# Two-batch transformer-and-state-space block on one core: setup work moved from ahead of batch 0 into its attention, x loaded early, two of three query spreading copies moved to POOL

## What is computed

```
0 attention: q, k, v = x@wq, x@wk, x@wv (16 query heads on 4 key heads, 16 wide), rotary;
             out = 0.5 * (softmax(causal) @ v + softmax(local, window 32) @ v);  out @ wo
1 feed-forward: w1, w2 = ternary(W_fc), ternary(W_proj)  (groups of 64 weights, scale = mean |w|)
             h = relu(x @ w1.T)**2;  rms_norm(h) @ w2.T
2 state-space mixer: in-projection, softplus time steps, 64 heads of 8, state 64, chunks of 64 tokens,
             gate silu(z), rms_norm, out-projection
3 rank mixer: x @ sum of 8 factors of 256x256, plus bias
```

## Time and profile before

| | |
|---|---|
| median of three runs (lowest, highest) | 1797.98 us (1793.96, 1803.11) |
| the profiled execution | 1803.51 us, of which its span is 1801.7 us |
| busy: PE, PEld, DVE | 1399.0 us (78%), 811.3 us (45%), 1166.2 us (65%) |
| busy: ACT, POOL | 924.9 us (51%), 277.8 us (15%) |
| mean granted TensorE clock | 0.861 of full speed |
| DMA | 63.29 MB, mean 35 GB/s |

### The profile page before, as it was taken

The page is one execution under the profiler, slowest core; times in us unless marked ns, Lnnn a source line. Parts: engine busy times, 40 slices in busy tenths (PEclk is TensorE's granted clock), DMA queues, the critical chain, the costliest instruction groups (busy, mean ns, idle before and its releaser), DMA issues.

```text
span 1801.7 us, 41575 instructions
## 1 busy us (share of the span) xinstructions
PE 1399.0 (78%) x15736; PEld 811.3 (45%) x15816; DVE 1166.2 (65%) x2039; ACT 924.9 (51%) x1557; POOL 277.8 (15%) x268
## 2 busy tenths in 40 slices
PE   0368898595789999998526789886866999999982
PEld 0253332142446666666425333322433666666652
DVE  7457773324558889987555577514255889888936
ACT  0282455432557777775307345552334777777640
POOL 7320000011112222221012000001102222222200
PEclk9678999888779999999858699987966999899996
DMA  5300000100142222220010000001005222222100
GB/s 168 101 1 3 2 2 2 47 0 13 45 86 58 50 53 52 47 54 18 1 49 1 2 2 2 2 1 47 12 1 118 49 48 58 47 47 58 37 1 24
DMA packets 36850, 63.29 MB, mean 35 GB/s; under 512 B 15073, under 2 KB 24033, under 8 KB 35953
## 3 DMA queue, kind: packets, MB, share of 16 engines
q1 hardware_dynamic: 36432, 59.48, 13.4%
q10 hardware_dynamic: 288, 2.10, 0.3%
HBM read 20.79 MB, written 7.01 MB: 15 GB/s over the span
## 4 chain that ended last, share of the span: by engine, by line
issue 68%; PE 15%; POOL 5%; POOLq 4%; DVE 4%; ACT 3%; DVEq 1%; DMA 0%; ACTq 0%; SPq 0%
POOL region L661 3%; PE PS L1588 2%; POOLq L643 2%; PE PS L1604 2%; PE PS L1573 2%; PE PS L1548 1%; POOL region L635 1%; PE PS L1621 1%; PE PS L1546 1%; PE PS L1644 1%; ACT L859 1%; PE PS L1692 1%; PE PS L1545 1%; PE PS L1627 1%; PE PS L1560 1%
## 5 line engine op out<-in xcount | busy, mean ns | idle before, releaser
L661 POOL TENSOR_TENSOR region<-region 128x1024 f32<-128x1024 f32 x64 | 152.6, 2384 | 531.7 <-DVE region L1198 531.7
L1069 DVE TENSOR_REDUCE region<-PS 128x1 f32<-128x512 f32 (+3 forms) x304 | 180.4, 652 | 80.3 <-PE PS L1374 44.0
L742 ACT ACTIVATE region<-PS 128x512 f32<-128x512 f32 x288 | 164.1, 597 | 128.5 <-PE PS L1421 87.2
L1310 PE MATMUL PS<-ident,S 128*128 128x128 f32 x128 | 35.0, 429 | 167.8 <-DVE S L966 164.8
L1588 PEld LDWEIGHTS PS<-region 64*64 64x64 f32 x4096 | 136.9, 135 | 40.7 <-issue 40.7
L1588 PE MATMUL PS<-region 64*64 64x64 f32 x4096 | 154.5, 224 | 0.0
L1371 PE MATMUL PS<-region 96*128 96x512 bf16 (+3 forms) x384 | 115.0, 350 | 24.1 <-DVE region L1069 15.9
L1421 PE MATMUL PS<-region 99*128 99x512 bf16 x288 | 113.4, 417 | 18.5 <-ACT region L742 17.5
L1195 DVE SCALAR_TENSOR_TENSOR region<-region,rows 128x1024 f32<-128x1024 f32 x64 | 82.2, 1284 | 66.6 <-PE PS L1627 48.2
L642 POOL TENSOR_TENSOR region<-region 128x512 f32<-128x512 f32 x28 | 35.4, 1265 | 553.5 <-ACT region L784 552.7
L851 ACT COPY region<-PS 128x512 f32<-128x512 f32 x128 | 74.7, 583 | 81.3 <-PE PS L1573 80.8
(11 more groups left out here) (258 smaller groups left out, 3000.0 us busy)
## 6 DMA issues: line engine op xcount, KB each, us to landing
region<-region SPq DMA_DIRECT2D x256, 128.0 KB, 2.3
region<-parts_scratch SPq DMA_DIRECT2D x8, 448.0 KB, 8.0
region<-in_L_ffn_factors_dram SPq DMA_DIRECT2D x2, 1024.0 KB, 7.1
X<-in_L_attn_x_dram SPq DMA_DIRECT2D x2, 1024.0 KB, 5.8
region<-w1T_scratch SPq DMA_DIRECT2D x2, 1024.0 KB, 4.9
region<-w2T_scratch SPq DMA_DIRECT2D x2, 1024.0 KB, 7.0
out_dram<-X SPq DMA_DIRECT2D x2, 1024.0 KB, 4.9
parts_scratch<-region SPq DMA_DIRECT2D x2, 768.0 KB, 3.2
```

Of the source, the lines that this page charges most:

```text
L661: nc.gpsimd.tensor_tensor(PB1[:, r], PB1[:, r], PB2, ALU.add).then_inc(s_bb, 1)
L742: nc.scalar.activation(PB[:, u % (2 * G0), :], PS[:, 2 + u % 2, :], ACT.Exp).then_inc(s_p, 1)
L1069: nc.vector.reduce_max(MB[:, h:h + nh, k0 // 4], src, AX).then_inc(s_smu, 1)
```

## The change

1. **Setup moves.** x of batch 0 is the first load; seven inputs that the attention needs follow on a semaphore of their own (`s_first`), then the rest (`s_w`), then the feed-forward weights. The batch loop is written out for both batches instead of being a hardware loop (the inner loops of the mixer stay). POOL makes the mixer's constants (`loop_constants`) and the ternary weights (`ternary_weights`, now all POOL, in quarters of 1024 elements, with a tree of additions for the mean) after the query and key stage of batch 0. PE and ACT transpose and copy the ternary weights at the end of batch 0's attention (`late_constants`), straight into `w1T` and `w2T`; only batch 1 loads them from DRAM. The factors load at the end of attention 0, and `fsum` is summed behind the next `norm_input`. The scaling of `w_out_s` stands in DVE's last "out1" step of batch 0.
2. **x early.** x of batch 1 is loaded into a buffer `XF` during the gating of batch 0's mixer. DVE's first `norm_input` of batch 1 reads `XF`; POOL copies it to `X` once the output of batch 0 has been stored.
3. **Spreading copies.** Of ACT's three spreading copies of the queries only the first (of `SP1`) stays; `SP2` twice and `SP3` once are spread by three more POOL copies, behind its six.

The core of the diff:

```diff
 SP
-            sp.dma_start(TW[:, 0]...).then_inc(s_wt, 16)
-            sp.dma_start(TW[:, 1]...).then_inc(s_wt, 16)
+            sp.dma_start(X[:], xv(0)).then_inc(s_x, 16)
...
+                sp.wait_ge(s_qxt, NT)
                 sp.dma_start(steps_f, steps_d).then_inc(s_kw, 16)
                 sp.dma_start(heads_f, heads_d).then_inc(s_kw, 16)
...
-            with sp.Fori(0, NB) as b:
-
-                sp.wait_ge(s_out, b * 16)
-                sp.dma_start(X[:], x[bass.ds(b, 1), :, :]...).then_inc(s_x, 16)
+            for b in range(NB):
...
+                if b == 0:
+                    loop_constants()
+
                 sp.wait_ge(s_s, b * BLOCKS * NT + NT)
+                if b == 0:
+                    sp.dma_start(fac[:, 0], factors[:, 0:P, :]...).then_inc(s_fac, 16)
+                    sp.dma_start(fac[:, 1], factors[:, P:, :]...).then_inc(s_fac, 16)
...
+                if b + 1 < NB:
+                    sp.wait_ge(s_gg, b * NT + 1)
+                    sp.dma_start(XF, xv(b + 1)).then_inc(s_x, 16)
 POOL
+            def ternary_weights():
+                pool.wait_ge(s_wt, 32)
...
+                for w, c, g in quarters:
+                    s = slice(c, c + 1024)
+                    nc.gpsimd.tensor_tensor(grp(TA[:, w, s]), grp(TWB[:, w, s]), wide(TH[:, w, g:g + 16]), ALU.subtract)
+                    nc.gpsimd.tensor_tensor(grp(TR), grp(TWB[:, w, s]), wide(TH[:, w, g:g + 16]), ALU.add)
+                    pool.drain()
+                    nc.gpsimd.tensor_scalar(TA[:, w, s], TA[:, w, s], 0.0, None, ALU.is_gt)
+                    nc.gpsimd.tensor_scalar(TR, TR, 0.0, None, ALU.is_lt)
+                    pool.drain()
+                    nc.gpsimd.tensor_tensor(TA[:, w, s], TR, TA[:, w, s], ALU.subtract)
...
+                pool.drain().then_inc(s_wq, 1)
...
+                if b > 0:
+                    pool.wait_ge(s_x, (b + 1) * 16)
+                    nc.gpsimd.tensor_tensor(X[:], XF, onesc[:].unsqueeze(2).to_broadcast([P, NT, C]), ALU.mult)
+                    pool.drain().then_inc(s_xf, 1)
...
+                    qx = QX[:, r, 0:H0]
+                    for dst, part in ((qx[:, :, 3:4, :], SP2), (qx[:, :, 4:5, :], SP2), (qx[:, :, 5:6, :], SP3)):
+                        nc.gpsimd.tensor_copy(dst, part[:, r, 0:H0, :].unsqueeze(2))
                     pool.drain().then_inc(s_qx, 1)
 
+                if b == 0:
+                    loop_constants()
+                    ternary_weights()
 ACT
-            act.wait_ge(s_w, 16 * NLOAD)
+            act.wait_ge(s_first, 16 * NFIRST)
...
-                        for dst, part in ((qx[:, :, 0:3, :], SP1), (qx[:, :, 3:5, :], SP2), (qx[:, :, 5:6, :], SP3)):
-                            last = nc.scalar.copy(dst, part[:, n % 2, 0:H0, :].unsqueeze(2).to_broadcast(list(dst.shape)))
-                        last.then_inc(s_qxq, 1)
+                        dst = qx[:, :, 0:3, :]
+                        nc.scalar.copy(dst, SP1[:, n % 2, 0:H0, :].unsqueeze(2).to_broadcast(list(dst.shape))).then_inc(s_qxq, 1)
...
+                if b == 0:
+                    late_constants()
                 transposed_input(b, 1)
 DVE
-            nc.vector.tensor_tensor(TW, TW, TA, ALU.subtract).then_inc(s_wq, 1)
...
+                norm_input(XF if b else X)
+                dve.wait_ge(s_first, 16 * NFIRST)
...
                 norm_input()
+                if b == 0:
+                    dve.wait_ge(s_fac, 32)
+                    nc.vector.tensor_reduce(fsum[:], fac.rearrange("p k r e -> p k e r"), AX, ALU.add).then_inc(s_fs, 1)
 PE
+            def late_constants():
+
+                pe.wait_ge(s_smu, npieces)
+                pe.wait_ge(s_p, nunits)
+                pe.wait_ge(s_og, NT)
+                pe.wait_ge(s_ex, 1)
...
+                pe.wait_ge(s_wq, 1)
...
+                if b == 0:
+                    late_constants()
                 transpose_input(b, 1)
```

More of the change, by code:

```diff
@@ L592, in _ @@
                 pool.drain()
[L593 to L594 removed]
+                for q in range(3):
+                    nc.gpsimd.tensor_copy(FP[:, q], FR)
                     pool.drain()
[L596 to L599 removed]
@@ new lines, in loop_constants @@
+                    for j in range(2):
+                        for half in range(2):
+                            nc.gpsimd.tensor_copy(FE[:, q, 4 * j:4 * j + 3, 64 * j + 32 * half:64 * j + 32 * half + ROT],
+                                                  FP[:, q, j].unsqueeze(1).to_broadcast([PAIRS, 3, ROT]))
+                pool.drain().then_inc(s_fe, 1)
+                pool.wait_ge(s_wb, 1)
+                nc.gpsimd.tensor_copy(NL[0:64], identb[0:64, 0:64].unsqueeze(1).to_broadcast([64, HEADS, Q]))
@@ L685, in _ @@
-            act.wait_ge(s_ex, 2)
-            nc.scalar.copy(rows[:], PS[:, 4, 0:4 * PAIRS].rearrange("p (k r) -> p k r", k=4)).then_inc(s_rp, 1)
-            for u in range(8):
-                act.wait_ge(s_wtp, u + 1)
-                nc.scalar.copy(TWT[:, u // 4, (u % 4) * 512:(u % 4 + 1) * 512], PS[:, u % 4, :]).then_inc(s_wtc, 1)
-            act.wait_ge(s_wtc, 8)
-            act.dma_start(w1T_d, TWT[:, 0]).then_inc(s_wts, 16)
-            act.dma_start(w2T_d, TWT[:, 1]).then_inc(s_wts, 16)
@@ L957, in root, with norm_input @@
                     dve.drain()
-            def norm_input():
+            def norm_input(X=X):
                 moments(X)
@@ L1101, in _ @@
                     elif kind == "out1":
+                        if b == 0 and i == NT - 1:
+                            dve.wait_ge(s_w, 16 * NLOAD)
+                            for k in range(DI // P):
+                                nc.vector.tensor_scalar(w_out_s[:, k, :], w_out_s[:, k, :], nw_s[:, k:k + 1], None, ALU.mult)
                         dve.wait_ge(s_ot, b * NT + i + 1)
@@ L1312, in transpose_input @@
                 pe.wait_ge(s_xt, b * BLOCKS * NT + (block + 1) * NT)
-            pe.wait_ge(s_rp, 1)
-            pe.wait_ge(s_wtc, 8)
-            with pe.Fori(0, NB) as b:
+            for b in range(NB):
                 transpose_input(b, 0)
```

324 lines of the change are left out of this document (172 added, 152 removed).

## The result

The changed kernel takes **1737.85 us** (median of 4 runs, 1732.74 to 1739.44) where the kernel before took 1800.55 in the same session: a ratio of **0.9649, with a 95% interval of 0.9612 to 0.9687**. The forecast was 1732, with 1716 to 1748 as its own range. The profiled execution took 1737.99 us, with a span of 1736.2. Medians in this document are over all executions of a kernel, ratios leave out two executions at a far lower granted clock (2512.12 us at 0.57 among the six of gated_copy, 1995.03 us at 0.68 among those of the kernel before).

What follows compares the result with a forecast made beforehand. Setup, then ACT in the query stage and PE and DVE alternating in attention were taken to bound it. 1803.5 - 64.8 - 9.3 - 10.8 + 18 = 1736.6 us, or 1732 against the median 1798.0; range 1716 to 1748.

Steps and rivals of the forecast that it cites:

- Setup, -64.8: Before batch 0: x loaded first lets DVE start at about 7.1 us instead of 71.9, saving 64.8 us.
- the late pieces: End of attention 0: PE's transposes, ACT's copies and the factor sum fit in idle gaps, taken as 0 us.
- POOL's chain: Ternary weights on POOL during attention 0: 106 us of work, 90 us of slack before PE asks for them.
- the soft one: POOL's price of 1.034 us per one-input instruction, taken from the nearest cast; at worst 5.7 us each.
- Contention, +18: Attention 0: DVE's short split instructions wait for POOL's long ones, adding 18 us, bounds 0 and 36.
- The rule that I weighed: Attention 0: shared-port lock makes every split instruction wait for a whole POOL instruction, 36 us; full-lock rival's chance 0.2.
- Spreading copies, -9.3: Query and key stage: moving copies from ACT to POOL saves 4.7 us a batch, 9.3 in all.
- 0.78 x 6 tiles: Query and key stage: ACT's tile falls from 5.05 to 4.27 us in six tiles, 4.7 us a batch.
- x early, -10.8: Between the batches: DVE's 10.79 us wait for x goes, saving 10.8 us; memsets may delay normalising 0 to 3.

Runs made afterwards that it cites:

- gated_copy: Changed kernel with POOL's chain split behind DVE's splits, batch 1's memsets behind DVE's normalising, copy of x behind the spreading copies; 1726.67 us, ratio 0.9588.
- POOL idle: Changed kernel with POOL's ternary-weight arithmetic left out, so the feed-forward gets unquantised weights; 1727.96 us, ratio 0.9623.
- store_held: Changed kernel with the store of the mixer's sources held until PE finished its transposes of B, C and the decays; 1740.34 us, ratio 0.9659.
- x_late: Changed kernel with x of batch 1 loaded into X only after batch 0's output is stored, without XF and POOL's copy; 1750.41 us, ratio 0.9711.
- spread_only: Kernel before with only the third part of the change, spreading copies of the queries' second and third parts on POOL; 1795.72 us, ratio 0.9975.
- gated: Changed kernel with POOL's chain cut into pieces, each waiting until DVE has finished a split step; 1734.33 us, ratio 0.9628.
- twice: Changed kernel with POOL's ternary arithmetic issued in batch 1's attention as well, on memory nothing reads; 1745.3 us, ratio 0.9695.
- pe_pad: Changed kernel with 224 always-fulfilled waits put into PE's program of each batch, ahead of its wait for B and C; 1739.95 us, ratio 0.9657.
- copy_one: Kernel of gated_copy with the spreading copy of the queries' third part back on ACT; 1725.73 us, ratio 0.9567.

## Why the prediction was right, point by point

**Setup, -64.8.** Measured -65.5. The seven loads behind x cost nothing that the stage shows (60.1 us to the first maximum, 61.9 before), and the late pieces at the end of attention 0 stayed hidden: from its last copy to the first squaring of the feed-forward 24.41 us, 24.44 before.

**POOL's chain.** It started at 82.3 us and ended at 207.1 instead of 188 (82.3 and the 106 forecast), for one price was wrong: each of the 16 TENSOR_SCALARs of 1024 elements took 2.77 us and not the 1.03 of the nearest cast; the prediction had called that price the soft one. With over 85 us of slack it cost nothing.

**Contention, +18.** Measured +15.5, and POOL idle takes it all away. The mechanism held: DVE's short instructions wait for POOL's, mostly one waits and one more passes in the gap, so a large split (one of five instructions) waits three times (5.3 us in the rows above). But the agreement of the sum is partly luck, since two things are in it, DVE's waits and the granted clock. Attentions at one clock tell them apart. Here are attention 1 of the kernel before, where POOL rests, and attention 0 of store_held and of x_late, where its chain is unbroken:

```profile
997.50:1215.70 218.20, 187.22 (x1664) 70.12 (x1669) 125.12 (x259) 100.13 (x192) 0.00 (x0) 0.89 0.01 2
67.40:289.90 222.50, 189.24 (x1676) 71.93 (x1673) 140.97 (x263) 100.49 (x192) 135.12 (x102) 0.89 0.03 8
67.50:293.10 225.60, 188.74 (x1677) 73.90 (x1676) 152.49 (x263) 100.86 (x192) 134.96 (x103) 0.89 0.03 8
```

At 0.89 they take 218.2, 222.5 and 225.6 us, and their split steps lose 0, 12.2 and 24.5 us to POOL. At 0.90 it is 215.6 and 215.7 with POOL at rest (both attentions of spread_only), 216.7 gated and 222.5 with the chain unbroken (attention 1 of twice, where the splits lost 14.1 us). At 0.88 it is 228.0 unbroken (pe_pad) and 222.1 gated (copy_one). So the 24.6 us lost in the splits cost the path some 6 to 7 us, and the rest of the 15.5, some 8 to 10, went with the clock, which no term of the sum has.

The term for the waits alone was thus two and a half to three times too large. What was mis-sized is the number of waits: the prediction took 5.3 us of each large split to the path, between three waits (3.3 us) and five (7.4 us). The three large splits that met the chain lost 5.3, 4.0 and 4.8 us, which leaves 2.5, 1.1 and 2.0 above PE's 2.84 us of slack. With 2.84 taken from each of the seven splits that POOL met, 8.5 of the 24.6 us remain, near the 7.4 between the attentions at 0.89: the slack was read rightly.

Why the clock was lower is open. In the sixteen attentions in which POOL's chain does not run it was 0.92 or 0.93 in thirteen, and 0.89, 0.90 and 0.90 in the other three, all in kernels without the new setup. In the eight with the chain unbroken it was 0.87 to 0.91, so that DVE's waits may help to lower it. But copy_one has 0.88 with next to no waits, and the kernel before 0.89 with none, so they are not its only cause.

The rule that I weighed, in the Trainium skill, page SBUF — State Buffer, section Who interferes with whom (an exclusive lock, held for a whole instruction), agrees with what a single row shows, 141.51 to 143.44. It does not agree with the rows at 173.57 and 174.51, where DVE ended a cast 1.71 us before POOL's TENSOR_SCALAR ended, and then ran a subtraction with two SBUF inputs wholly inside it; here the measurement decides. As a price for the path the rule gave 36 us, and the path paid a fifth of that: not all five instructions of a split waited, PE's slack took much of what did, and some waits ended early.

**Spreading copies, -9.3.** Measured -3.3. ACT's tile became 4.16 us (4.27 forecast). What failed is "0.78 x 6 tiles": four steps are paced by it, and PE's first transposes wait longer for POOL, whose nine copies I had held to be under 3.3 us a tile with room to spare. The first tile's took 3.5 us (27.77 to 31.27), and PE's first transposes start behind them, at 31.42. So the attention proper began at 66.6 us and not near 63.

**x early, -10.8.** Measured -7.1. DVE's wait of 10.79 us went, and 3.7 of it came back: POOL's memsets and copy held DVE's normalising for 5.3 us, where I had allowed 0 to 3 and put 0 into the sum.

**Not forecast.** +10.1 us in the preparation of the mixer, some 3.4 a batch from PE's stops and 1.7 from the matmuls at the low clock behind them, and about -15 us in batch 1 and the mixers, where the granted clock rose (attention 1 from 0.89 to 0.92). The four forecast terms came to -60.4 where -66.9 was said, and what I had not forecast added -5.1 in all. That the total came so near is partly luck.

## What to carry over

POOL's work, moved under DVE's, was charged by the length of the single instruction that DVE met (for TENSOR_SCALARs by the first 1.06 us of it, for the most part), and at the dependent short instructions that PE waits for. So place such work between those: with a wait on their semaphore, 135 us of POOL's work cost about 1 us at equal clock (216.7 us against 215.6 at 0.90), and attention 0 of gated_copy was as short as with POOL idle. (That of copy_one, gated too, took 222.1 us at 0.88, a clock at which no attention with POOL at rest was seen.) Or cut it into shorter pieces (218.0 us). A forecast should state what the granted clock was in the stretch it uses, and check a measured term at equal clock before it is called confirmed.

## What was unexpected about the hardware

- On POOL a TENSOR_SCALAR of 128x1024 took 2.77 us in bf16 and in f32, longer than a TENSOR_TENSOR of the same size with a broadcast operand (1.90 us) and than a cast (1.0 us).
- Eight DVE TENSOR_SCALARs of 128x256, 2.67 us in all, took 7.98 us beside POOL memsets, which read nothing, and one POOL instruction of 3.73 us.
- A POOL TENSOR_SCALAR of 128x1024 lasts 2.77 us in the profile but held DVE's short instructions only until 1.06 us after its start; until 1.89 us all of them ran at 0.17 to 0.18 us.
- PE stopped in the middle of a run of transposes for 1.1 to 4.5 us, at the same instruction in the changed kernel and ten variations of it, with nothing in the profile that it waited for.
- The same matmuls of attention 0 kept PE busy for 181.2 us (granted clock 0.92) to 192.6 us (0.87).
